# Attention and last stage as one block of programs, with the first tiles of the last stage prepared inside attention

## The reference

```
qkv = x @ Wqkv;  q (32 heads of 32), k (32), v (32)
probs = softmax(q k^T / sqrt(32) + slope_h * (pos_k - pos_q), causal)
y = layernorm(x + (probs v) @ Wo)
out = layernorm(y + y @ w_q^T + bias)      # w_q: int4 fake quantization of the weight
```

## Time and profile before

| what | before |
|---|---|
| median of 3 runs | 2315.71 us (2315.28 to 2316.40) |
| the profiled execution | 2316.04 us |
| its span | 2314.3 us |
| PE busy | 2248.7 us, 97% of the span |
| DVE busy | 1602.9 us, 69% |
| ACT busy | 986.4 us, 43% |
| POOL busy | 906.5 us, 39% |
| granted PE clock, mean | 0.987 |

### The profile page before, as it was taken

The page is one execution under the profiler, slowest core; times in us unless marked ns, Lnnn a source line. Parts: engine busy times, 40 slices in busy tenths (PEclk is TensorE's granted clock), DMA queues, the critical chain, the costliest instruction groups (busy, mean ns, idle before and its releaser), DMA issues. The chain is left out here.

```text
span 2314.3 us, 36451 instructions
## 1 busy us (share of the span) xinstructions
PE 2248.7 (97%) x12536; PEld 1531.1 (66%) x12536; DVE 1602.9 (69%) x4970; ACT 986.4 (43%) x1950; POOL 906.5 (39%) x558
## 2 busy tenths in 40 slices
PE   7999999899999999999999999978999999999997
PEld 6888888655555555555555555537888888888886
DVE  6977677867778777887787778825555555555554
ACT  4222222057777777777777777741111010101010
POOL 0000000047878787778777877740101010101110
PEclk9999999989999999999999999989999999999999
DMA  6555554543442443243323322245323333332310
GB/s 227 185 185 197 197 191 152 138 118 91 107 105 73 107 107 94 79 112 98 79 67 94 89 72 74 57 150 177 105 82 99 90 91 93 88 99 82 100 64 28
DMA packets 179295, 257.06 MB, mean 111 GB/s; under 512 B 15446, under 2 KB 104918, under 8 KB 178762
## 3 DMA queue, kind: packets, MB, share of 16 engines
q1 hardware_dynamic: 178966, 254.87, 38.0%
q10 hardware_dynamic: 180, 0.33, 0.0%
HBM read 166.89 MB, written 87.20 MB: 110 GB/s over the span
## 5 line engine op out<-in xcount | busy, mean ns | idle before, releaser
L234 DVE CUSTOM_DVE_ANT_0 xm<-pa,xm 128x128 bf16<-128x128 f32 (+1 forms) x1488 | 748.8, 553 | 216.6 <-PE pa L215 212.6
L1155 ACT ACTIVATE probs<-pa,slope 128x512 f32<-128x512 f32 (+3 forms) x1536 | 765.6, 592 | 247.9 <-PE pa L1053 107.3
L1023 POOL TENSOR_TENSOR probs<-probs 128x1024 f32<-128x1024 f32 x252 | 673.8, 2674 | 85.3 <-ACT probs L1155 66.9
L1378 POOL TENSOR_TENSOR yb<-y,xm 128x1024 f32<-128x1024 f32 x32 | 76.7, 2398 | 661.8 <-DVE z L1401 639.5
L1069 PE MATMUL pa<-probs,v 128*32 128x512 f32 (+3 forms) x3072 | 299.6, 492 | 0.5 <-DMA q<-xm 0.2
L1342 ACT ACTIVATE ln<-ln 128x1 f32<-128x1 f32 x64 | 13.0, 203 | 504.8 <-DVE ln L1421 504.8
L1009 POOL TENSOR_SCALAR_AFFINE_SELECT probs<-probs 128x512 f32<-128x512 f32 x256 | 158.5, 637 | 150.6 <-ACT probs L1155 150.6
L1289 PE MATMUL pf<-fo_hi,at_hi 128*128 128x512 f32 x512 | 203.2, 397 | 14.1 <-DVE at_lo L1393 13.3
L1289 PE MATMUL pf<-ff_lo,xk 128*128 128x512 f32 x512 | 203.2, 397 | 0.0
L1289 PE MATMUL pf<-fo_hi,at_lo 128*128 128x512 f32 x512 | 200.4, 391 | 0.0
L1289 PE MATMUL pf<-fo_lo,at_hi 128*128 128x512 f32 x512 | 200.3, 391 | 0.0
(11 more groups left out here) (145 smaller groups left out, 3767.2 us busy)
## 6 DMA issues: line engine op xcount, KB each, us to landing
xm<-in_L_attn_hidden_states SPq DMA_DIRECT2D x8, 2048.0 KB, 9.2
q_hi_d<-q_hi SPq DMA_DIRECT2D x64, 256.0 KB, 2.0
q_lo_d<-q_lo SPq DMA_DIRECT2D x64, 256.0 KB, 2.5
att_d<-att SPq DMA_DIRECT2D x64, 256.0 KB
xm<-in_L_attn_hidden_states SPq DMA_DIRECT2D x32, 512.0 KB, 3.7
out<-z SPq DMA_DIRECT2D x32, 512.0 KB, 2.6
q<-q_hi_d SPq DMA_DIRECT2D x62, 256.0 KB, 6.0
xq<-q_hi_d SPq DMA_DIRECT2D x44, 256.0 KB, 5.7
```

What stands on the lines that cost most here:

```text
L234: nc.vector.tensor_tensor_reduce(out=unused[:, 0:keys], in0=bank[:, 0:keys], in1=sh.distance[:, d0:d0 + keys], scale=1.0, scalar=-3e38, op ...
L1023: nc.gpsimd.tensor_tensor(o, o, probs[:, source % PR, h0:h1, 0:N], ALU.add).then_inc(add_done, 1)
L1155: nc.scalar.activation(probs[:, n % PR, h, 0:N], sc_ps[sc_ring.bank[use]][:, at:at + N], ACT.Exp, scale=slope[:, bass.ds(g * HPG + h, 1)]) ...
L1378: nc.gpsimd.tensor_tensor(yb[:, :], y[:, u, :], bias[:, :], ALU.add).then_inc(yb_done, 1)
```

## The change

`attend` and `finish` no longer open blocks of their own: each returns its five programs, and `layer` opens one block in which every engine runs the one and then the other. What one needs of the other goes through an object `Seam` (buffers and semaphores). In detail:

- The sums of batch 0 alone (8 steps, `EARLY = ITS - LATE = 8`) are read back, inverted on DVE (128x256 elements, at step 30 after unit 3's maximum) and stored, in step 30. The other 24 steps' sums (128x768 elements) are read back, inverted and stored inside `finish`, by SP at tiles 0 and 1 and by DVE at the end of tile 1's work.
- In step 31 SP loads the attended values and reciprocals of tiles 0 and 1 and x of tiles 0 and 1 (`first_tiles`, 12 DMAs), then stores step 30's second half, and only then loads the high half of the weight.
- DVE and ACT normalize and split tile 0 behind their last step of attention, and DVE normalizes tile 1, before DVE's last `evacuate`; tile 1 is split at the start of `finish`.
- In `finish`, SP, ACT and POOL first wait until all products of attention are done (`pv_done`). SP then issues `ff_lo`, the last stores of attention, the bias and tile 2's attended values; it waits for all stores of attention before it reads the late sums.
- `linear` waits for the first turned half before its half 0, for the second one in the middle of it, and for z's two halves one by one.
- After the loop, ACT's `turned_hi(31)` and DVE's `turned_lo(31)` come ahead of the second norm of tile 30.
- Some buffers move (`yt_lo`, `at_hi`, `at_lo`, `recip`).

The diff, cut to its core:

```diff
+        a = attend(nc, ctx, sh, seam, x, rows_d, q_hi_d, q_lo_d, k_d, v_d, att_d, sums_d, recip_d, wo_d, wf_d)
+        f = finish(nc, ctx, sh, seam, x, bias, att_d, sums_d, recip_d, wf_d, out)
+        block = ctx.enter_context(nc.Block())
...
-        early = sh.early[0:EARLY * HPG, :]
+        EARLY = ITS - LATE
+        early = seam.late[:, 0, :]
...
+            def first_tiles(sp):
+                sp.wait_ge(seam.recip_stored, 16)
+                x_v = tokens.rearrange("b s h -> (b s) h").rearrange("(t p) h -> p t h", p=P)
+                memory = ((sh.at_first, sh.recip_first), (seam.at_second[:, :, :], seam.recip_second))
+                for n, (at_in, recip) in enumerate(memory):
+                    load_attended(sp, att_d, recip_d, at_in, recip, seam.at_loaded[n], n)
+                for n in range(2):
+                    sp.dma_start(sh.x3[n][:, None, :], x_v[:, n:n + 1, :]).then_inc(seam.x_loaded[n], 16)
+            def half_of_third(sp):
+                for n, mem in enumerate((sh.xq, seam.q2)):
+                    src = wf_d[0, :, n * KT // 2:(n + 1) * KT // 2, :].rearrange("p k (a q) -> p (k a) q", q=CH)
+                    sp.dma_start(raw(mem[:, :, :]), src).then_inc(seam.w3_in[2], 16)
...
+                if before_last:
                     for c in range(HALF):
                         sp.wait_ge(att_stored[c], EARLY * 32 + CREDIT)
                     sp.dma_start(early, early_d[0]).then_inc(sums_back, 16)
+                if last:
+                    first_tiles(sp)
+                if not first:
+                    put_att(sp, t - 1, 1)
+                if before_last:
+                    sp.wait_ge(recip_done, 1)
+                    sp.dma_start(early_d[1], early).then_inc(seam.recip_stored, 16)
+                if last:
+                    half_of_third(sp)
                 put_att(sp, t, 0)
-                if last:
-                    sp.wait_ge(recip_done, 1)
-                    sp.dma_start(early_d[1], early).then_inc(recip_stored, 16)
-                    sp.wait_ge(recip_stored, 16)
-                    load_attended(sp, att_d, recip_d, sh.at_first, sh.recip_first, at_loaded[0], 0)
                 if not last:
                     put_max(sp, sh, q3[(u + 1) % SLOTS], t + 1, 0, mx_use[t + 1, ("turn", 0)] + 1)
...
-            put_att(sp, ITS - 1, 1)
-            for c in range(HALF):
-                sp.wait_ge(att_stored[c], 32 * ITS + CREDIT)
-            sp.dma_start(late[:, :], late_d).then_inc(late_in, 16)
...
             every_step(ITS, SLOTS, body)
+            split_hi(nc, act, seam, sh.at_hi_first, sh.at_first, 0)
             take_sums(ITS - 1, 1)
...
-                    if last and n == BPH:
+                    if t == ITS - 2 and n == 3:
                         dve.wait_ge(sums_back, 16)
                         nc.vector.reciprocal(early, early).then_inc(recip_done, 1)
             every_step(ITS, SLOTS, body)
+            normalize(nc, dve, seam, sh.at_first, sh.recip_first, 0, 0)
+            split_lo(nc, dve, seam, sh.at_lo_first, sh.at_first, sh.at_hi_first, 0)
+            normalize(nc, dve, seam, seam.at_second[:, :, :], seam.recip_second, 1, 0)
             evacuate(ITS - 1, 1)
...
             sp.dma_start(raw(wf_lo_all[:, :, :]), wf_d[1]).then_inc(wf_lo_in, 16)
+            seam.put_last_att(sp)
             sp.dma_start(bias[:, :], bias_h[None, :].to_broadcast([P, H])).then_inc(bias_in, 16)
-            sp.wait_ge(late_done, 1)
-            sp.dma_start(recip_d[B * NG - 4:B * NG].rearrange("t h (a q) -> (t h a) q", q=P), late[:, :]).then_inc(recip_stored, 16)
...
-                    load_x(t + 1, 1 - u)
+                    if not first:
+                        load_x(t + 1, 1 - u)
                 if not last and not before_last:
                     load_at(t + 2, u)
-                if first:
+                if t == 0:
+                    for c in range(HALF):
+                        sp.wait_ge(seam.att_stored[c], 32 * ITS + CREDIT)
+                    sp.dma_start(seam.late[:, :, :], late_d[0]).then_inc(seam.late_in, 16)
+                elif t == 1:
+                    sp.wait_ge(late_done, 1)
+                    sp.dma_start(late_d[1], seam.late[:, :, :]).then_inc(recip_stored, 16)
+                elif t == 2:
                     sp.wait_ge(recip_stored, 32)
...
+        def tensor(pe):
+            def product(ps, done, lhs, rhs, h, second=None):
                 for k in range(KT):
+                    if second and k == KT // 2:
+                        pe.wait_ge(*second)
...
             def linear(t, u):
-                pe.wait_ge(yt_lo_done, t * 2 + 2)
-                pe.wait_ge(z_sum, t * HV)
-                if isinstance(t, int) and t == 0:
+                first = isinstance(t, int) and t == 0
+                if first:
                     pe.wait_ge(w3_in[2], 32)
                     pe.wait_ge(wf_lo_in, 16)
                 for h in range(HV):
-                    product(f_ps, f_done, (yt_hi, yt_lo), (wf_hi, wf_lo), h)
+                    if not first:
+                        pe.wait_ge(z_sum, t * HV - 1 + h)
+                    if h == 0:
+                        pe.wait_ge(yt_lo_done, t * 2 + 1)
+                    product(f_ps, f_done, (yt_hi, yt_lo), (wf_hi, wf_lo), h, (yt_lo_done, t * 2 + 2) if h == 0 else None)
...
-            split_hi(0, 0, True)
+            act.wait_ge(seam.pv_done, seam.blocks)
+            split_hi(nc, act, seam, at_hi[1], at_in[1], 1)
...
+                if not first and not last:
+                    split(t + 1, 1 - u)
                 root(t, 0)
             edge_loop(act, NT, body)
+            turned_hi(NT - 1)
             root(NT - 2, 1)
-            turned_hi(NT - 1)
...
+        def gpsimd(pool):
+            pool.wait_ge(seam.pv_done, seam.blocks)
             for u in range(2):
                 pool.memset(credit[:, u:u + 1], 0.0).then_inc(stored[u], CREDIT)
             pool.wait_ge(bias_in, 16)
+            for c in range(HALF):
+                pool.wait_ge(seam.att_stored[c], 32 * ITS + CREDIT)
...
-            normalize(0, 0, 0)
-            split_lo(0, 0)
-            normalize(1, 1, 0)
-            split_lo(1, 1)
-            dve.wait_ge(late_in, 16)
-            nc.vector.reciprocal(late[:, :], late[:, :]).then_inc(late_done, 1)
+            split_lo(nc, dve, seam, at_lo[1], at_in[1], at_hi[1], 1)
+            def invert_late():
+                dve.wait_ge(seam.late_in, 16)
+                nc.vector.reciprocal(seam.late[:, :, :], seam.late[:, :, :]).then_inc(late_done, 1)
...
-                    normalize(t + 1, 1 - u, i + u)
+                    normalize(nc, dve, seam, at_in[1 - u], recip[1 - u], 1 - u, i + u)
...
-                    split_lo(t + 1, 1 - u)
+                    split_lo(nc, dve, seam, at_lo[1 - u], at_in[1 - u], at_hi[1 - u], t + 1)
                 if not first:
                     z_half(t - 1, 1 - u, i if u == 1 else i - 1, 0)
+                if second:
+                    invert_late()
             edge_loop(dve, NT, body)
+            turned_lo(NT - 1)
             z_half(NT - 2, 0, NT // 2 - 1, 1)
             norm(NT - 2, 0, 1)
-            turned_lo(NT - 1)
```

More of the change, by code:

```diff
@@ L12 @@
 from concourse import mybir
+from collections import namedtuple
 from contextlib import ExitStack
@@ L273, in layer, with _ @@
         q2 = ctx.enter_context(nc.sbuf_tensor("q2", [P, KT, CH], f32r))
[L274 to L280, removed]
+        k2 = ctx.enter_context(nc.sbuf_tensor("k2", [P, S], f32r))
+        at_second = ctx.enter_context(nc.sbuf_tensor("at_second", [P, KT, P], fp32))
+        late = ctx.enter_context(nc.sbuf_tensor("late", [P, B - 1, NG * HPG * S // P], fp32))
+        seam = Seam(nc, ctx, fo, q2, k2, at_second, late)
+        a = attend(nc, ctx, sh, seam, x, rows_d, q_hi_d, q_lo_d, k_d, v_d, att_d, sums_d, recip_d, wo_d, wf_d)
+        f = finish(nc, ctx, sh, seam, x, bias, att_d, sums_d, recip_d, wf_d, out)
+        block = ctx.enter_context(nc.Block())
+        @block.sync
+        def _(sp):
+            a.sync(sp)
+            f.sync(sp)
+        @block.gpsimd
+        def _(pool):
+            a.gpsimd(pool)
+            f.gpsimd(pool)
+        @block.tensor
+        def _(pe):
+            a.tensor(pe)
+            f.tensor(pe)
+        @block.scalar
+        def _(act):
+            a.scalar(act)
+            f.scalar(act)
+        @block.vector
+        def _(dve):
+            a.vector(dve)
+            f.vector(dve)
 def project(nc, sh, x, wqkv, wo, wf, qscale_h, distance_h, qrows_h, krows_h, ident_h, slope_h, rows_d, q_hi_d, q_lo_d, k_d, v_d, wo_d, wf_d):
@@ L969, in body @@
                     n, k = divmod(t - 2, KT)
-                    sp.dma_start(raw(fo[n][:, k:k + 1, :]), wo_d[n, :, k:k + 1, :]).then_inc(w3_in[n], 16)
-                if last:
-                    for n, mem in enumerate((sh.xq, q2)):
-                        src = wf_d[0, :, n * KT // 2:(n + 1) * KT // 2, :].rearrange("p k (a q) -> p (k a) q", q=CH)
```

(21 more changed lines are left out.)

121 lines of the change are left out of this document (61 added, 60 removed).

## The result

The median of 4 runs after is 2297.32 us (2296.52 to 2300.81), against 2315.64 (2315.28 to 2316.40) before: the ratio is 0.9926 (95% interval 0.9914 to 0.9938), 18.3 us less. Forecast were 27.9 us less.

The account below looks back on a forecast made before the run. PE, busy 97% of the span, bounds the kernel, so only its stops and slow-clock stretches can be won. Terms -13.0 - 2.3 - 4.4 - 2.2 - 3.9 - 2.4 + 0.3 = -27.9 us give 2287.8 us; range 2284 to 2298.

Parts of the forecast that it names:

- attention to its last product: Step 30 of attention: DVE's added 128x256 reciprocal delays PE's maxima by between 0 and 1.75 us, taken as +0.3.
- idle at the seam: Between attention's last product and the first Wo matmul: PE's idle 13.25 us become some 0.25, -13.0 us.
- first tile's Wo: First 48 Wo matmuls after attention: run at full clock because PE no longer stops, -2.3 us.
- stop before the first linear: PE's 4.93 us wait before the first linear: 0.5 remains as tile 2's load lands early enough, -4.4 us.
- its slow stretch: 72 matmuls after the stop before the first linear: fall from 18.81 to 16.58 us, -2.2 us.
- 29 full tiles, last 72 matmuls: Last stage's tiles: 96 matmuls plus turn still take 22.89 us a tile, so no term in the sum.
- stop at the end: Before the last linear: PE starts at 2289.8 instead of 2293.71, as the turned tile is split earlier, -3.9 us.
- last 48 matmuls: Last linear: 11.0 plus 0.2 us instead of 13.69, at full clock after a shorter stop, -2.4 us.
- What costs nothing: Last stage: late reciprocal, SP's waits at tiles 0 and 1, and two more waits a tile in `linear` cost nothing.
- rival 1: First linear: tile 2's load is late, a 7.9 us stall plus 2.2 of slow clock, 2297.4 us; chance 0.12.
- slack of 2.6 us: First linear: tile 2's load lands at 1563.0, where landing by 1565.6 would cost nothing.
- 63 waits in `linear`: Last stage: two more waits a tile in `linear`, 63 in all, cost nothing since existing waits show no cost.

Follow-up runs that it names:

- e1: Changed kernel plus three unused pads so every operand of the last stage's matmuls starts at a multiple of 512 bytes: 2285.56 us, ratio 0.9871 to before.
- e2: Kernel before the change with only `at_hi` and `at_lo` moved to 96 bytes past a multiple of 512: 2327.26 us, ratio 1.0049.
- e3: Changed kernel with the old waits of `linear`, all before its first matmul and none inside: 2301.67 us, ratio 0.9937 to before.
- e4: Changed kernel plus 416 unused bytes before `ff_lo`, putting `ff_lo`, `at_hi`, `at_lo`, `yt_lo` at 0 while `xq`, `xk` stay at 128: 2296.93 us, ratio 0.9916.
- g3: Changed kernel with tile 2's attended values and reciprocals loaded by ScalarE's queue instead of SP's: 2300.49 us, ratio 0.9925 to before.
- g4: Changed kernel itself run again, unmodified, as base for the other runs of its round: 2299.67 us, ratio 0.9925 to before.
- g2: Changed kernel where VectorE waits for GpSimd's last addition of attention before normalizing tile 0: 2298.55 us, ratio 0.9923 to before.
- f1: Kernel before the change with only the new waits in `linear` and the new order at the end: 2308.55 us, ratio 0.9973.
- f4: Kernel before the change with attended values of even tiles at 64 and odd tiles at 256 bytes past a multiple of 512: 2319.93 us, ratio 1.0022.
- g1: Changed kernel with last-stage operands at one place modulo 512, VectorE waiting for GpSimd's addition, and ScalarE loading tile 2: 2279.48 us, ratio 0.9840 to before.
- f2: Kernel before the change with two pads (384 bytes ahead of `xq`, 128 behind `mx1`) putting all operands at 0 modulo 512: 2305.09 us, ratio 0.9958.
- f3: Kernel before the change with one 128-byte pad ahead of `fo_hi`, putting all last-stage operands at 128 modulo 512: 2309.08 us, ratio 0.9973.

## Why the prediction was wrong

Terms as forecast, and between the two profiled executions:

| term | forecast | measured | from |
|---|---|---|---|
| attention to its last product | +0.3 | +1.2 | 1543.32 to 1544.48 |
| idle at the seam | -13.0 | -13.3 | 13.25 to none |
| first tile's Wo | -2.3 | -2.0 | 14.31 to 12.31 up to tile 1 |
| stop before the first linear | -4.4 | -3.8 | 4.93 to 1.11 |
| its slow stretch | -2.2 | -1.9 | 18.81 to 16.87 |
| **29 full tiles, last 72 matmuls** | **0** | **+7.5** | 22.89 to 23.15; 16.58 to 16.71 |
| stop at the end | -3.9 | -3.7 | 4.85 to 1.18 |
| last 48 matmuls | -2.4 | -2.4 | 13.69 to 11.32 |
| all | -27.9 | -18.1 | spans 2314.3 to 2296.2 |

(The rest, +0.3, is tile 1's own matmuls.)

**The step that failed** is the one under "What costs nothing": that linear and turn would "still" be 22.89 us a tile. I read the moved buffers as a matter of who overwrites whom and gave them no term, neither a value nor a bound. Measured, that term is +7.5 us, of the 9.8 by which the two traces miss the sum. PE is the bound in 31 tiles, so the term that is multiplied by 31 was the one to be careful with. e1 and e2 show the cause from both sides, by moving buffers alone: it is the places of the operands, and with them the tile has become 0.26 us longer (0.29 more in the two Wo halves, 0.03 less in `linear`). The prediction's own test, "wrong if the tile's period has changed", caught it. With this term as measured the sum is 2295.3, inside the range. That the measured 2297.3 is nearly the 2297.4 of rival 1, which the range had been stretched to take in, is chance: that rival's stall of 7.9 us did not come.

**Attention's end, +1.2 for +0.3.** Step 30 cost nothing (1.75 us, no idle ahead of it); the cost is in step 31, where I had put the multiplication of tile 0 "long before 1538" at no price. It started 0.5 us into an addition of GpSimd and ended 1.1 us behind that one's end, 5.15 us for 1.22; GpSimd's next addition then took 5.32 for 4.56, and PE's last products wait for that one. From the last but one `evacuate` to the last product's end are 22.32 us before and in e2, and 22.75 to 22.77 in e3, e4, g3 and g4: 0.4 us, and g2 (22.68) shows that waiting does not save it. The other 0.8 of the 23.53 in the profile after goes with a dip of the clock and is not the change's: f1 to f4, with the attention of the kernel before, have 23.50 to 23.56, and a dip as well. f1's, columns as in the table of stretches:

```profile
1528.00:1532.00 4.00, 3.53 (x11) 1.42 (x14) 0.00 (x0) 4.00 (x8) 3.83 (x2) 0.84 0.23 65
1532.00:1536.00 4.00, 3.68 (x20) 1.06 (x12) 3.89 (x1) 2.67 (x6) 1.97 (x2) 0.73 0.18 68
```

e1 has it (23.58), and the kernel before, e2, e3, e4 and g1 to g4 do not. Why the clock fell in six of the fourteen profiles is open.

**The first linear.** Right in kind, late by 5 us: the landing is at 1568.2, not 1563.0. The queue was not empty when attention ended. SP's issues and the table of landings of the changed kernel:

```profile
1518.44 6.40 SPq L1271 DMA_DIRECT2D k<-recip_d  x4
...
1530.21 0.74 SPq L1021 DMA_DIRECT2D q<-wf_d  x1
```

```profile
q<-wf_d SPq DMA_DIRECT2D x1, 2048.0 KB, 15.7
```

The weight's high half was issued at 1530.2, since SP needed 6.4 us for four loads, and landed at 1545.9, where I had 1540. The rate was as I took it: the Trainium skill's bound of 358 GB/s ("DMA: Bandwidth & Descriptors", "Where 436 GB/s comes from") is exceeded at 1532 to 1536 with 436. The slack of 2.6 us was gone, 1.1 of stop remained, and 2.3 in g4. This was rival 1 in a small form; its 7.9 us were far from it.

**The end.** 1.18 us of stop for 0.9, and the matmuls behind it at full pace. (The prediction's own figures, 13.69 less 11.2, give 2.5 for the last term, not 2.4.) The Trainium skill's warning ("TensorE: Matmul & The Clock Gate", "A second HAM failure mode: psum-queue depth-cycling") would have taken the 2.4 us back; a stop of 1.18 after work without a hole did not, here and in f1. The late reciprocal, SP's waits and the 63 waits in `linear` were free, as forecast (e3).

## What to carry to other kernels

Where PE sets the time, a tensor added, removed or resized anywhere ahead of matmul operands can change what each matmul costs. So look at the offsets of both operands whenever a change touches buffers, and multiply by the number of tiles. Here 512 bytes of padding by themselves took 9.8 us off the kernel before (f2), about half of what the rewrite of two stages gave. With all operands at one place modulo 512, which takes 928 bytes, the changed kernel ran another 18 to 20 us faster (g1); some 8 of them the change itself had cost. And a small load that was issued behind large ones landed when they had landed; another queue did not help it (g3).

## What the runs showed of the hardware

- 24 fp32r matmuls (128x128 loaded, 128x512 moving) that follow one another without a stop took 5.45 us, 227 ns each, where the places in SBUF of the two operands were 0 or 256 bytes apart, and 5.58 to 5.62 us where they were 64, 96 or 128 apart (e1, f3, f4; e2, f4 and the kernel after). Whether the shared place was 0 or 128 made no difference (f2, f3).
- The 48 matmuls of `linear` took 10.88 us with all operands at one place (e1, f2, f3, g1) and 11.07 to 11.15 with mixed ones. Among mixed ones a matmul took 228 to 233 ns even with its own two operands at one place (the kernel before, e4).
- A VectorE multiplication of two SBUF operands, 128x1024, takes 1.22 us alone. Started 0.5 us into a GpSimd addition of 4.56 us it took 5.15, and the addition that followed took 5.32 (the kernel after; in g4 5.32 and 5.33).
- Four loads of 128 KB in pieces of 512 bytes held the issuing queue for 11 to 14 us while the DMA engines were full, on SP (13.20 in the kernel after, 11.76 in g4) as on ScalarE (13.88 in g3), and for 2.2 us at 1515.66 in the kernel after, when they were not.
- After single stops of 0.88 to 1.59 us in otherwise unbroken work PE's granted clock stayed at 1.00; after 2.29 us it was 0.66 over the next 4 us (g4), after 2.23 us still 1.00 (e3).
